# Moving the first chunk's quantisation into the scan's tail, a rounding step in PSUM, and attention's head before a stage boundary

## The chip, the cores and the metric

The kernel runs on one core of one Trainium2 chip. The metric is the device time of one execution in microseconds; the time before is 1036.28 us, the median of three runs (1035.46 to 1037.93).

## The reference

The input x has 8 sequences of 256 tokens with 128 features. Four residual blocks follow one another, each on a layer-normalised input:

```python
x = x + mamba4(layernorm(x))     # 4 mamba layers: projection, causal conv of 4 taps, silu,
                                 # selective scan h = exp(d*A)*h + d*u*B ; y = sum(h*C) + u*D,
                                 # y * silu(z), projection; 256 channels x 16 states
x = x + ffn(layernorm(x))
x = x + attention(layernorm(x))  # 16 heads of 8, causal, position bias, softmax, projection
x = x + ffn(layernorm(x))        # the same weights
```

The feed-forward block quantises to FP4 in blocks of 16 along the last dimension, the input, the weights and the hidden values:

```python
scale = max(abs(block)) / 6      # then nearest of 0, .5, 1, 1.5, 2, 3, 4, 6 with sign, times scale
gate, y = fp4(x) @ fp4(w_gate).T, fp4(x) @ fp4(w_up).T       # 352 columns each
out = fp4(silu(gate) * y) @ fp4(w_down).T
```

## The kernel before

All of x stays in SBUF (`resid`, 16 tiles of 128 tokens by 128 features). A chunk is four tiles (512 columns), a feed-forward step (k = 0 to 7) is two tiles (704 hidden columns). The kernel writes each engine's queue by hand; every engine works through its queue in order and waits on semaphores. The four stages are separate blocks, and an engine starts the next block after a barrier.

**The scan (`mamba_stage`).** There are 16 pairs of sequences-by-layer (n), each with 16 sub-steps (k). In a sub-step TensorE (PE) injects inputs into PSUM, ScalarE (ACT) computes four decays three sub-steps ahead, VectorE (DVE) runs four scans (L902), GpSimd (POOL) multiplies by C (L1002), and PE sums the products over the states into PSUM (L567). Behind sub-step 4 of the next pair DVE gates the result (`gating`, L911); for the last layer `add_out` (L917) adds the output projection to `resid` behind sub-step 9. After the last sub-step of the last pair, DVE computes the moments (L1038, L1042) of chunks 0 to 2 for the norm of FFN1, their offsets (L1065), then gates and adds the last output. ACT computes the reciprocal deviation (`scalar_rstd`: Ln and Exp) and normalises three chunks (L1073).

**The rounding (`Rounder`).** For one chunk or step: DVE takes peak (L1104), scale (L1106), reciprocal (L1108), a factor just below one (L1110); POOL multiplies (`pool_normal`, L1116); DVE takes the exponent bits (L1124); ACT makes the rounding step of them (L1130); DVE adds and subtracts it (`vector_round`, L1137 and L1139); POOL multiplies by the scale (`pool_dequant`, L1144). Value and step are SBUF tiles.

**FFN1 and FFN2 (`ffn_stage`).** Four x chunks are quantised, transposed by PE into a PSUM bank (L1360) and copied by ACT (L1423). Each tile has a gate matmul (L1370) and an up matmul (L1372), two banks each; ACT applies silu (L1430), DVE multiplies (L1270, `hidden`), then h is rounded, transposed (L1380), copied (L1435, L1436), multiplied by the down weights (L1390, two banks in turn) and added to `resid` by DVE (`add`, L1278). DVE rounds step k-2 and adds step k-5 during step k. In FFN2 three chunks of x are already quantised during attention; in FFN1 none is.

**Attention's head.** At the end of FFN1 chunk 0 is normalised and transposed for attention, and two of four groups of strips (`tensor_strips` L1617, `vector_strips` L1628) are computed. The other two groups and the values of chunk 0 (`project_v` L1707, `values` L1836), and POOL's constants (L1923 to L1927), stand at the head of the attention block, before the first scores (L1714, L1723).

Of the kernel before, what the change touches and what calls it, by code (L numbers as in the profile page):

```python
# [13 lines left out]
P = 128  # L14
F32 = mybir.dt.float32
BF16 = mybir.dt.bfloat16
# [203 lines left out]
def mamba_stage(core, x, w_xi, w_z, w_xp, w_dt, w_out, chan, ident_in, c_rows, diag_rows, w_ffn, norm):  # L220
# [3 lines left out]
    core.minus_step = core.sb("minus_step", [P, 1])  # L224
    with ExitStack() as stage:
# [87 lines left out]
        with nc.Block(no_gpsimd_drain=True) as block:  # L313
# [335 lines left out]
            def _(a):  # L649
# [142 lines left out]
                for n in range(NPAIR):  # L792
                    more = n + 1 < NPAIR
                    for k in range(SUBS):
# [10 lines left out]
                        if k == 13 and more:  # L805
                            read_dut(n + 1, 0)
                            read_dut(n + 1, 1)
                        decays(n * SUBS + k + 3)
# [21 lines left out]
                for c in range(PAIRS - 1):  # L830
                    norm.scalar_rstd(a, c)
                for c in range(PAIRS - 1):
                    norm.scalar_normalise(a, c)

            @block.vector
            def _(v):
# [81 lines left out]

                first_stats(0)
# [32 lines left out]
                for c in range(PAIRS - 1):  # L952
                    ring.wait_read(v, "out", NPAIR - PAIRS + c)
                    norm.vector_moments(v, c)
                for c in range(PAIRS - 1):
                    norm.vector_offset(v, c)
                gating(NPAIR - 1)
                add_out(NPAIR - 1)

            @block.gpsimd  # L960
            def _(p):
# [47 lines left out]
                for n in range(NPAIR):  # L1009
                    for k in range(SUBS):  # L1010
# [3 lines left out]
                        if k == 11 and n % PAIRS == 1 and lay(n) + 1 < DEPTH:  # L1014
                            layer_weights(lay(n) + 1)

# [61 lines left out]
class Rounder:  # L1078


    def __init__(self, core, sb, tag, blocks, depth=2):
        self.core, self.blocks, self.depth = core, blocks, depth
# [3 lines left out]
        self.value = sb(f"{tag}_value", [P, depth, blocks * BLK])  # L1086
# [6 lines left out]
        self.s_dequant = core.sem(f"{core.stage}_{tag}_dequantised")  # L1093

# [17 lines left out]
    def pool_normal(self, p, src, c):  # L1112
# [3 lines left out]
        self.core.nc.gpsimd.tensor_tensor(self.blocked(self.value[:, i, :]), src, self.spread(self.inv[:, i, :]),  # L1116
                                          ALU.mult).then_inc(self.s_normal, 1)

    def vector_exponent(self, v, c):
        i = c % self.depth  # L1120
        v.wait_ge(self.s_normal, c + 1)
        if c >= self.depth:
            self.s_round.wait(v, "rounded", c - self.depth)
        self.core.nc.vector.tensor_scalar(self.step[:, i, :].bitcast(U32), self.value[:, i, :].bitcast(U32), EXP_BITS, None,  # L1124
                                          ALU.bitwise_and).then_inc(self.s_exponent, 1)

    def scalar_step(self, a, c):
        i = c % self.depth
        a.wait_ge(self.s_exponent, c + 1)
        self.core.nc.scalar.activation(self.step[:, i, :], self.step[:, i, :], ACT.Relu, bias=self.core.minus_step[:, :],  # L1130
                                       scale=HALF_STEP).then_inc(self.s_step, 1)

    def vector_round(self, v, c):
        nc, i = self.core.nc, c % self.depth
        value, step = self.value[:, i, :], self.step[:, i, :]
# [972 lines left out]
```

## Time and profile before

| what | value |
|---|---|
| runs | 1035.46, 1036.28, 1037.93 us |
| the profiled execution | 1035.28 us |
| its span | 1033.6 us |
| busy: PE, DVE, ACT, POOL | 949.8, 902.6, 761.5, 760.9 us |
| scan, to the last add_out | up to 727.7 us |
| FFN1, to the last add | 728.1 to 802.4 us |
| attention | about 807 to 967 us |
| FFN2, to the last add | 967.6 to 1031.2 us |

The time of the execution holds the span and what lies around it. The stages' limits are read off the timeline at the lines named above. Busy shares are averages over stages with different limits, so each place that the change touches has to be read by itself.

### The profile page before, as it was taken

What the parts mean: (1) busy time and instruction counts of PE and PEld (TensorE: products, weight loads), DVE (VectorE), ACT (ScalarE), POOL (GpSimd) and SP (SyncE); (2) the same over time, 40 slices, a digit from 0 to 9 for tenths busy, and PEclk for the clock granted to TensorE, in tenths of its full rate; (3) what the DMA queues carried; (4) which work ended last, traced back from release to release, by engine and by line L of the source; (5) the groups of instructions that cost most, each with busy time, mean ns of one, the idle gap of its engine ahead of it and who ended that gap; (6) DMA issues with size and microseconds to landing.
All of it is one profiled execution on the core that took longest, in us unless ns stands there. A gap on an engine that the chain in (4) does not pass through costs nothing. (4 is left out here: it accounts for less than half of the span.)

```text
span 1033.6 us, 29750 instructions
## 1 busy us (share of the span) xinstructions
PE 949.8 (92%) x11909; PEld 580.2 (56%) x11909; DVE 902.6 (87%) x1724; ACT 761.5 (74%) x1683; POOL 760.9 (74%) x426
## 2 busy tenths in 40 slices
PE   5799999999999999999999999988477999999786
PEld 2455555565555555555555555655346566666456
DVE  6879998999989999899998999999699767787597
ACT  5888898988989889899898897984434255555442
POOL 1688999989999899999999989998254223333243
PEclk9799999999999999999999999999888999999888
DMA  6745453544535444454444544440571010000001
GB/s 187 254 160 166 137 173 125 166 147 162 167 128 164 147 165 146 145 167 146 165 146 138 158 147 159 147 132 14 128 155 21 21 23 17 7 2 2 1 0 41
DMA packets 69272, 120.88 MB, mean 117 GB/s; under 512 B 40072, under 2 KB 51152, under 8 KB 60112
## 3 DMA queue, kind: packets, MB, share of 16 engines
q1 hardware_dynamic: 69136, 118.98, 37.3%
q8 instruction: 95, 1.56, 0.6%
q14 instruction: 41, 0.34, 0.1%
HBM read 111.10 MB, written 6.29 MB: 114 GB/s over the span
## 5 line engine op out<-in xcount | busy, mean ns | idle before, releaser
L902 DVE TENSOR_TENSOR_SCAN hid<-decay,acc 128x256 f32<-128x256 f32 x1024 | 604.6, 664 | 40.9 <-PE acc L539 40.4
L1002 POOL TENSOR_TENSOR prod<-hid,c_rep 128x1024 f32<-128x1024 f32 x256 | 600.7, 2380 | 43.8 <-DVE hid L902 32.9
L765 ACT ACTIVATE decay<-delta,a_neg 128x255 f32<-128x255 f32 x1024 | 428.4, 502 | 47.6 <-DVE hid L902 47.4
L539 PE MATMUL acc<-b_diag,du_t 64*64 64x256 f32 x4096 | 273.1, 383 | 15.9 <-DVE hid L902 12.2
L567 PE MATMUL ring<-prod,ident 64*64 64x256 f32 x4096 | 255.5, 379 | 2.2 <-POOL prod L1002 2.2
L539 PEld LDWEIGHTS acc<-b_diag,du_t 64*64 64x64 f32 x4096 | 147.9, 134 | 124.8 <-DVE hid L902 55.3
L567 PEld LDWEIGHTS ring<-prod,ident 64*64 64x64 f32 x4096 | 152.0, 133 | 83.5 <-issue 22.7
L1916 POOL TENSOR_SCALAR_AFFINE_SELECT att_probs<-att_probs 128x512 f32<-128x512 f32 x64 | 41.1, 642 | 102.5 <-ACT att_probs L1959 100.1
L1959 ACT ACTIVATE att_probs<-acc 128x384 f32<-128x384 f32 x128 | 55.8, 488 | 52.5 <-PE acc L1733 52.5
L444 PE MATMUL ring<-xpad,diag_cw 64*64 64x512 f32 x512 | 60.5, 589 | 0.0
L1116 POOL TENSOR_TENSOR ffn_h_value<-ffn_h,ffn_h_inv 128x704 f32<-128x704 f32 x16 | 23.7, 1480 | 43.2 <-DVE ffn_h_value L1139 32.5
L1130 ACT ACTIVATE ffn_h_step<-ffn_h_step,minus_step 128x704 f32<-128x704 f32 x16 | 14.1, 883 | 54.7 <-DVE ffn_h_step L1124 54.7
L1731 PE MATMUL acc<-att_qk 17*128 17x256 f32 x256 | 53.2, 426 | 0.5 <-ACT att_probs L1959 0.4
L1723 PE MATMUL ring<-att_qk 17*128 17x256 f32 x256 | 47.3, 426 | 0.0
L1845 DVE TENSOR_REDUCE att_npk<-ring 128x2 f32<-128x512 f32 x64 | 43.7, 683 | 0.0
L1370 PE MATMUL ring<-wgT,ffn_xqT 128*128 128x352 f32 x64 | 30.0, 556 | 14.8 <-ACT ffn_silu L1430 9.2
L1844 DVE TENSOR_REDUCE att_npk<-ring 128x2 f32<-128x256 f32 x64 | 27.1, 423 | 16.6 <-PE ring L1722 16.3
L989 POOL TENSOR_TENSOR du<-delta,u 128x512 f32<-128x512 f32 x30 | 37.7, 1285 | 0.0
L1733 PE MATMUL acc<-att_qk 17*128 17x128 f32 x256 | 33.1, 269 | 0.0
L444 PEld LDWEIGHTS ring<-xpad,diag_cw 64*64 64x64 f32 x512 | 19.8, 133 | 22.6 <-issue 19.1
L427 PE MATMUL ring<-cur,wxi 128*128 128x512 f32 x60 | 31.5, 650 | 0.8 <-ACT cur L659 0.8
L1733 PEld LDWEIGHTS acc<-att_qk 17*128 17x128 f32 x256 | 31.7, 185 | 0.8
(180 smaller groups left out, 1263.7 us busy)
## 6 DMA issues: line engine op xcount, KB each, us to landing
c_rep<-c_rows SPq DMA_DIRECT2D x64, 1024.0 KB, 4.7
b_diag<-diag_rows SPq DMA_DIRECT2D x62, 512.0 KB, 3.9
diag_rows<-zeros SPq DMA_DIRECT2D x2, 2048.0 KB, 12.4
att_qk<-in_pos_q SPq DMA_DIRECT2D x4, 768.0 KB
att_qk<-in_pos_k SPq DMA_DIRECT2D x4, 768.0 KB
att_qk<-att_dense SPq DMA_DIRECT2D x24, 64.0 KB
resid<-in_x SPq DMA_DIRECT2D x4, 256.0 KB, 3.9
c_rows<-bc SPq DMA_DIRECT2D x64, 8.0 KB, 1.5
```

The costliest lines, as they stand in the source:

```text
L444: last = nc.tensor.matmul(out[h * HALF:(h + 1) * HALF, :], diag_cw[rows, lay(n) % 2, h, k, :], xpad[rows, h, :, k:k + SEQ], start=(k == 0) ...
L539: last = nc.tensor.matmul(inj[m * HALF:(m + 1) * HALF, K % 2, at:at + HALF * SG], du_t[rows, n % 2, e, chans:chans + HALF], b_diag[rows, K ...
L567: last = nc.tensor.matmul(y[h * HALF:(h + 1) * HALF, at], ident[rows, rows], prod[rows, H % PRODS, h, s, :], start=False, stop=(H % HSUMS ...
L765: last = nc.scalar.activation(decay[:, K % DECAYS, s, 1:], delta[:, n % 2, h, e * SEQ + 1:(e + 1) * SEQ], ACT.Exp, scale=a_neg[:, lay(n) % ...
L902: last = nc.vector.tensor_tensor_scan(hid[:, K % HIDS, s, :], decay[:, K % DECAYS, s, :], rows[:, s, :], 0.0, ALU.mult, ALU.add)
L1002: nc.gpsimd.tensor_tensor(prod[:, K // 2 % PRODS, h], hid[:, K % HIDS, :, :], c_rep[:, g, :, at], ALU.mult).then_inc(s_prod, 1)
L1723: return nc.tensor.matmul(out[:, P:SPAN], q[:, P:], k, start=False, stop=True, skip_group_check=True)
L1731: nc.tensor.matmul(out[:, 0:SEQ], k[:, 0:P], q, start=True, stop=True)
L1733: banks.fill(nc.tensor.matmul(out[:, SEQ:SPAN], k[:, P:], q[:, P:], start=True, stop=True), f"t{i}", u)
L1845: last = nc.vector.tensor_reduce(npk[:, g % 2, 1, at], score_bank(u)[:, :, P:SPAN], AX, ALU.max, negate=True)
L1916: nc.gpsimd.affine_select(at, at, [[0, 4], [1, P]], ALU.is_ge, zero, base=0, channel_multiplier=-1).then_inc(s_causal, 1)
L1959: banks.read(nc.scalar.activation(probs[:, g % 3, js[i], 0:SPAN], banks.bank(f"t{i}", u)[:, 0:SPAN], ACT.Exp, scale=SCALE), f"t{i}", u)
```

## The change

Nothing of what is computed changes. What moves is:

- **Scan's tail.** In the last pair DVE computes the moments of chunk 0 behind sub-step 6, the offset of chunk 0 behind 9, the moments of chunk 1 behind 12. Behind the last scan it quantises chunk 0 (its multiply on DVE, by a new `vector_normal`), with offset 1, the moments of chunk 2 and the rounding before the last gating. POOL dequantises chunk 0 at its queue's end.
- **Rounder.** The x chunks are rounded in place in `normed`. For h, ACT writes its step to PSUM (704 columns, one buffer), and so DVE's two rounding instructions read one operand from there.
- **FFN.** One gate bank rather than two; one down bank rather than two; the transposes of x and of h share a bank. DVE rounds step k-1 during step k, adds step k-4 between the maxima and the rounding, and takes the exponent of the step before ahead of the products. POOL's dequantisation waits for that exponent. In both stages ACT loads silu's table before it copies chunk 0.
- **Attention's head.** All four strip groups, the values of chunk 0 and POOL's constants stand at FFN1's end.

```diff
+                        if n == NPAIR - 1:
+                            if k in (6, 12):
+                                chunk_moments(k // 6 - 1)
+                            if k == 9:
+                                norm.vector_offset(v, 0)
+                first.vector_scales(v, 0)
+                first.vector_normal(v, 0)
+                first.q.vector_exponent(v, 0)
+                norm.vector_offset(v, 1)
+                chunk_moments(2)
+                first.q.vector_round(v, 0)
                 gating(NPAIR - 1)
+                norm.vector_offset(v, 2)
                 add_out(NPAIR - 1)
...
+    def vector_normal(self, v, src, c):
+        i = c % self.depth
+        self.s_scales.wait(v, "below", c)
+        need(v, self.s_dequant, c - self.depth + 1)
+        self.core.nc.vector.tensor_tensor(self.blocked(self.value(c)), src, self.spread(self.inv[:, i, :]),
                                           ALU.mult).then_inc(self.s_normal, 1)
...
     def scalar_step(self, a, c):
         i = c % self.depth
         a.wait_ge(self.s_exponent, c + 1)
-        self.core.nc.scalar.activation(self.step[:, i, :], self.step[:, i, :], ACT.Relu, bias=self.core.minus_step[:, :],
+        if self.held is not None and c:
+            self.s_round.wait(a, "rounded", c - 1)
+        self.core.nc.scalar.activation(self.steps(i), self.step[:, i, :], ACT.Relu, bias=self.core.minus_step[:, :],
...
-        gate_bank = [bank(ring, 1), bank(ring, 2)]
-        up_bank = [bank(ring, 3), bank(acc, 0)]
-        hT_bank = [bank(acc, 1)[:, 0:2 * P], bank(acc, 1)[:, 2 * P:4 * P], bank(acc, 2)[:, 0:2 * P]]
-        down_bank = [bank(acc, 3)[:, 0:2 * P], bank(ring, 0)[:, 0:2 * P]]
+        qh = Rounder(core, sb, "h", HCOLS // BLK, 4, acc[:, 2 * BANK:2 * BANK + HCOLS])
+        x_bank, gate_bank, up_bank = bank(ring, 0), bank(ring, 1), [bank(ring, 2), bank(acc, 0)]
+        hT_bank = [bank(ring, 0)[:, 0:2 * P], bank(ring, 0)[:, 2 * P:4 * P], bank(acc, 1)[:, 0:2 * P]]
+        down_bank = bank(ring, 3)[:, 0:2 * P]
...
+                norm.vector_moments(v, 3)
+                if early == 1:
                     x.vector_scales(v, 1)
+                    x.q.vector_exponent(v, 1)
                     x.vector_scales(v, 2)
+                norm.vector_offset(v, 3)
+                for k in range(HSTEPS + 1):
+                    if k >= 2:
+                        qh.vector_exponent(v, k - 1)
+                    if k == 2:
+                        x.q.vector_exponent(v, 3)
+                    if attention and k == HSTEPS - 1:
+                        v.wait_ge(s_add, 2)
+                        attention.norm.vector_moments(v, 0)
                     if k < HSTEPS:
                         hidden(k)
+                    if k >= 4:
+                        add(k - 4)
+                    if k == 0 and early == 1:
+                        x.q.vector_round(v, 1)
+                        x.q.vector_exponent(v, 2)
+                    if k == 1:
+                        qh.vector_exponent(v, 0)
                         x.vector_scales(v, 3)
+                    if attention and k == HSTEPS:
                         attention.norm.vector_normalise(v, 0)
+                    if k >= 1:
+                        qh.vector_round(v, k - 1)
+                    if k == 1 and early == 1:
+                        x.q.vector_round(v, 2)
+                    if k == 2:
+                        x.q.vector_round(v, 3)
...
+                for k in range(HSTEPS + 2):
+                    if k >= 2:
+                        p.wait_ge(qh.s_exponent, min(k, HSTEPS))
+                        h_dequant(k - 2)
+                    if k < HSTEPS:
+                        h_normal(k)
...
-                        need(t, s_silu, n - 1)
+                        need(t, s_silu, n)
...
-                    need(t, s_add, k - 1)
+                    need(t, s_add, k)
...
+                norm.scalar_rstd(a, 3)
+                nc.scalar.preload_act_table_set(SILU)
+                copy_x(0)
+                if early == 1:
                     x.q.scalar_step(a, 1)
                 gate(0)
+                norm.scalar_normalise(a, 3)
+                for k in range(HSTEPS + 2):
                     if 1 <= k <= HSTEPS:
                         qh.scalar_step(a, k - 1)
+                    if k == 0 and early == 1:
+                        x.q.scalar_step(a, 2)
...
-                for g in range(2, HGROUPS):
-                    tiles.tensor_strips(t, g)
-                project_v(0)
                 t.wait_ge(s_maskb, 2)
```

## Rows read from the trace of the kernel before

**Rows 1.** The page, part 1: busy us, share and instructions of each engine.
```profile
PE 949.8 (92%) x11909; PEld 580.2 (56%) x11909; DVE 902.6 (87%) x1724; ACT 761.5 (74%) x1683; POOL 760.9 (74%) x426
```

**Rows 2.** Timeline, scan's end: start us, us, engine, line, operation, out<-in, count, [idle before].
```profile
704.47 0.69 DVE L917 TENSOR_TENSOR resid<-resid,ring 128x512 f32<-128x512 f32 x1 [0.86 <-PE ring L514]
705.08 13.97 DVE L902 TENSOR_TENSOR_SCAN hid<-decay,acc 128x256 f32<-128x256 f32 x24
707.57 13.97 POOL L1002 TENSOR_TENSOR prod<-hid,c_rep 128x1024 f32<-128x1024 f32 x6 [1.45 <-DVE hid L902]
718.96 0.84 DVE L1038 BATCH_NORM_STATS2 stats<-resid 128x6 f32<-128x128 f32 x4
...
720.14 0.84 DVE L1038 BATCH_NORM_STATS2 stats<-resid 128x6 f32<-128x128 f32 x4
...
723.62 1.23 DVE L911 TENSOR_TENSOR yg<-ring,gate 128x1024 f32<-128x1024 f32 x1 [0.21 <-PE ring L567]
```

**Rows 3.** Timeline, one middle step of FFN2.
```profile
1006.82 1.39 POOL L1144 TENSOR_TENSOR ffn_hq<-ffn_h_value,ffn_h_scale 128x704 f32<-128x704 f32 x1
...
1007.55 0.70 DVE L1106 TENSOR_SCALAR ffn_h_scale<-ffn_h_peak 128x44 f32<-128x44 f32 x1
...
1008.84 0.52 DVE L1124 TENSOR_SCALAR ffn_h_step<-ffn_h_value 128x704 uint32<-128x704 uint32 x1
...
1009.28 0.88 DVE L1137 SCALAR_TENSOR_TENSOR ffn_h_value<-ffn_h_step,ffn_h_value 128x704 f32<-128x704 f32 x1
...
1011.17 1.39 POOL L1116 TENSOR_TENSOR ffn_h_value<-ffn_h,ffn_h_inv 128x704 f32<-128x704 f32 x1 [2.96 <-DVE ffn_h_value L1139]
1011.34 0.51 DVE L1270 TENSOR_TENSOR ffn_h<-ffn_silu,ring 128x352 f32<-128x352 f32 x1
...
1012.32 0.89 DVE L1104 TENSOR_REDUCE ffn_h_peak<-ffn_h 128x44 f32<-128x704 f32 x1
...
1013.24 0.70 DVE L1106 TENSOR_SCALAR ffn_h_scale<-ffn_h_peak 128x44 f32<-128x44 f32 x1
```

**Rows 4.** Timeline, attention: the offset beside POOL.
```profile
911.40 0.64 POOL L1916 TENSOR_SCALAR_AFFINE_SELECT att_probs<-att_probs 128x512 f32<-128x512 f32 x1 [1.87 <-ACT att_probs L1959]
...
911.70 0.36 DVE L1065 SCALAR_TENSOR_TENSOR ffn_offset<-meanvar,rstd 128x4 f32<-128x4 f32 x1
```

**Rows 5.** Timeline, the front of FFN1.
```profile
728.14 0.69 DVE L1104 TENSOR_REDUCE ffn_x_peak<-normed 128x32 f32<-128x512 f32 x1 [0.40 <-PEq L313]
...
729.56 0.86 DVE L1038 BATCH_NORM_STATS2 stats<-resid 128x6 f32<-128x128 f32 x4
...
731.20 0.20 ACT L1050 ACTIVATE rstd<-lnvar 128x4 f32<-128x4 f32 x1
...
733.63 1.28 ACT L1447 ACT_TABLE_LOAD   x1
...
736.76 0.60 ACT L1423 ACTIVATE ffn_xqT<-ring 128x512 f32<-128x512 f32 x1 [1.85 <-PE ring L1360]
...
740.16 0.46 ACT L1430 ACTIVATE ffn_silu<-ring 128x352 f32<-128x352 f32 x1 [2.19 <-PE ring L1372]
```

**Rows 6.** Timeline: FFN1's last add, FFN2's first DVE instruction and last add.
```profile
802.01 0.42 DVE L1278 TENSOR_TENSOR resid<-resid,ring 128x256 f32<-128x256 f32 x1 [0.46 <-PE ring L1390]
...
967.58 0.87 DVE L1038 BATCH_NORM_STATS2 stats<-resid 128x6 f32<-128x128 f32 x4 [0.39 <-PEq L1678]
...
1030.82 0.42 DVE L1278 TENSOR_TENSOR resid<-resid,ring 128x256 f32<-128x256 f32 x1 [0.92 <-PE ring L1390]
```

**Rows 7.** Timeline, FFN2's tail: down products on PE.
```profile
1024.52 2.77 PE L1390 MATMUL ring<-wdT,ffn_hqT 128*128 128x128 f32 x12
...
1029.28 1.50 PE L1390 MATMUL ring<-wdT,ffn_hqT 128*128 128x128 f32 x12
```

**Rows 8.** Windows: length, busy us (count) by engine, granted clock, DMA share, GB/s.
```profile
1000.00:1004.00 4.00, 3.86 (x21) 2.87 (x22) 3.86 (x8) 1.13 (x4) 2.52 (x2) 1.00 0.01 2
...
1024.00:1026.00 2.00, 2.00 (x11) 1.99 (x10) 1.14 (x2) 0.86 (x2) 1.05 (x1) 0.50 0.04 8
```

More of the change, by code:

```diff
@@ L807, in _ @@
                             read_dut(n + 1, 1)
+                        if k == 8 and not more:
+                            norm.scalar_rstd(a, 0)
                         decays(n * SUBS + k + 3)
@@ L829, in _ @@
                             a_rates(lay(n) + 1)
[L830 to L833, printed above, removed]
+                norm.scalar_normalise(a, 0)
+                norm.scalar_rstd(a, 1)
+                first.q.scalar_step(a, 0)
+                norm.scalar_normalise(a, 1)
+                norm.scalar_rstd(a, 2)
+                norm.scalar_normalise(a, 2)
             @block.vector
@@ L1085, in __init__ @@
         self.inv = sb(f"{tag}_inv", [P, depth, blocks])
-        self.value = sb(f"{tag}_value", [P, depth, blocks * BLK])
+        self.values = values or [self.value_tile(sb, tag, n) for n in range(depth)]
         self.step = sb(f"{tag}_step", [P, depth, blocks * BLK])
@@ L1152, in __init__ @@
         self.core, self.norm = core, norm
-        self.q = Rounder(core, sb, "x", CH // BLK)
-        self.xq = sb("xq", [P, CHUNKS, CH])
         self.normed = core.normed[:, :, :].rearrange("p t (b k) -> p (t b) k", k=BLK)
+        rows = core.normed[:, :, :].rearrange("p t d -> p (t d)")
+        self.q = Rounder(core, sb, "x", CH // BLK, values=[rows[:, c * CH:(c + 1) * CH] for c in range(CHUNKS)])
     def blocks(self, c):
@@ L1213, in scalar, with ffn_stage @@
         return last
-def ffn_stage(core, tag, norm, inputs=None, attention=None, out=None):
+def ffn_stage(core, tag, x, early, attention=None, out=None):
     nc, ring, acc, ident = core.nc, core.ring, core.acc, core.ident
@@ L1628, in vector_strips, with tensor_values, vector_values, pool_set @@
             banks.read(nc.vector.tensor_tensor(at, at, src, ALU.add), kind, 0)
+    def tensor_values(self, t, c):
+        nc, banks = self.core.nc, self.banks
+        banks.wait_free(t, "v", c)
+        banks.wait_read(t, "x", c)
+        for i in range(CH_TILES):
+            last = nc.tensor.matmul(banks.bank("v", c)[:, i * P:(i + 1) * P], self.xT[:, i * P:(i + 1) * P], self.wqkv[:, 2, :],
+                                    start=True, stop=True)
+        banks.fill(last, "v", c)
+    def vector_values(self, v, c):
+        nc, banks = self.core.nc, self.banks
+        banks.wait_filled(v, "v", c)
+        dst = self.vals[:, c * CH_TILES:(c + 1) * CH_TILES, :, 0:HD]
+        src = banks.bank("v", c).rearrange("p (t h d) -> p t h d", t=CH_TILES, d=HD)
+        bias = self.bv[:, :].rearrange("p (h d) -> p h d", d=HD).unsqueeze(1).broadcast_to([P, CH_TILES, HEADS, HD])
+        banks.read(nc.vector.tensor_tensor(dst, src, bias, ALU.add), "v", c)
+    def pool_set(self, p):
+        nc = self.core.nc
+        self.wait(p)
+        nc.gpsimd.tensor_copy(self.ident_b[:, :], self.core.ident[:, :]).then_inc(self.s_maskb, 1)
+        nc.gpsimd.tensor_copy(self.mask_b[:, :, :], self.mask[:, :].unsqueeze(1).broadcast_to([P, 2, P])).then_inc(self.s_maskb, 1)
+        nc.gpsimd.memset(self.npk[:, :, :, :], 0.0).then_inc(self.s_npk, 1)
+        nc.gpsimd.memset(self.vals[:, :, :, HD:HD + 1], 1.0).then_inc(self.s_ones, 1)
 def attention_stage(core, tiles, x):
```

228 lines of the change are left out of this document (86 added, 142 removed).

## The prediction

> **What bounds the kernel now.** I read the page's busy shares first: no engine fills the span, VectorE (DVE) has 902.6 us of 1033.6 [rows 1], so the answer lies in the stages. The edits touch three places: the last pass of the scan, the first feed-forward stage (FFN1) with its hand-over to attention, and the last one (FFN2). I then read the timeline of each.
>
> In the scan's end DVE and POOL run in lockstep. The last six sub-steps are 24 scans in 13.97 us, 2.33 us each, with no gap; POOL's six products take 13.97 us too, and start only after a scan [rows 2]. POOL's first product here starts 2.49 us after DVE's first scan, and its last ends at 721.54, 2.49 us after DVE's last scan at 719.05. So whatever is put between scans moves the end of the scan by its full length. Behind the scans, DVE computes the moments of chunks 0 to 2 while POOL's last product and TensorE's (PE's) last sums run; gating starts at 723.62, that is 4.57 us after the last scan, and it alone sets the end. Those moments are free today.
>
> In both FFN stages DVE is the bound of a middle step: from one scale instruction to the next is 5.69 us, with DVE never idle [rows 3]. In it lies a stall: the scale (128x44) takes 0.70 us where the exponent, sixteen times its size, takes 0.52. It ends at 1008.25, when POOL's dequantisation (1006.82 + 1.39 = 1008.21) has just ended. The same is seen on a four-element instruction in attention: it begins at 911.70 beside a POOL instruction and ends at 912.06, when POOL has just ended at 912.04 [rows 4]. The tensor_reduce, and the product with an operand in PSUM, keep their 0.89 and 0.51 us beside POOL [rows 3].
>
> **Part 1: chunk 0 quantised in the scan's tail.**
> Added between scans: moments(0) behind sub-step 6, offset(0) behind 9, moments(1) behind 12. One moments group is 1.18 us (718.96 to 720.14) [rows 2]; two are 2.4. The offset is a four-element instruction with both inputs in SBUF. POOL's product 9 starts when product 8 ends, about 0.15 us behind scan 9, and runs 2.33 us; after add_out (0.86 us of waiting, then about 0.6) the offset can start some 1.5 us behind scan 9 and by the attention rows waits for the product's end: about 1.0 us. If it didn't wait it would cost 0.15. I take 1.0, since the nearest row is the same instruction. Sum: the last scan ends 3.4 us later (bounds 2.5 and 3.6). ScalarE (ACT) gets a log and an exp of 0.5 us together in front of a decay; it is busy 74% of the span [rows 1], and I take nothing.
>
> Added between the last scan and gating: peak, scale, reciprocal, product, exponent, offset(1), moments(2), two roundings. The peak takes 0.7 us; the scale is then held until POOL's product ends, 2.49 us behind the scan. From there: scale, reciprocal and last factor about 0.65, the product of 512 columns 0.75 (the multiply of 704 columns that has two SBUF inputs takes 0.88 [rows 3]), exponent 0.5, offset 0.2, moments 1.2, roundings 1.5. That makes 7.1 us. Gating could have started at 4.57, so it is 2.5 us late. If nothing were held: 5.5 us, 0.9 late; were the roundings held by ACT's step too: 3.5 late. I take 2.5. Offset(2) goes behind gating, where DVE waits for PE.
> So FFN1 starts 3.4 + 2.5 = 5.9 us late (bounds 3.4 and 7.1).
>
> The Trainium skill's "SBUF — State Buffer", section "Who interferes with whom", says that VectorE and GpSimd share one port pair under an exclusive lock, which a VectorE instruction needs if it has two SBUF inputs or runs in a two-port mode; the loser waits for the whole instruction. By that rule offset(0) and the first scale wait as above; if the short rows were chance, the sum would be 3.4 instead of 5.9. The trace agrees with the rule in the rows named, and it is what speaks against this edit.
>
> **Part 2: FFN1's front.** Today from the stage's first DVE instruction (728.14) to the first silu (740.16) are 12.02 us, since chunk 0 is quantised there [rows 5]. After: moments(3), log and exp (729.56 to 731.40, 1.84 us), the table load (1.28), then copy of x to silu (736.76 to 740.16, 3.40): 6.5 us. Of the 5.9 lost, 5.5 come back here at first. But one gate bank means that the second tile's gate matmul waits for the first silu: 0.5 us of silu, then one tile on PE. At half clock such a tile is most of the 3.40 us from copy to silu, some 2.4; at full clock I take half of it, 1.2. The second silu comes some 2.5 to 3 us behind the first. It delays DVE by about 2.1 us at the first step and 1.5 at the second. And the order of queues holds more: ACT's step of chunk 2 stands before the gates of step 1, and waits for an exponent which stands behind the first step and the rounding of chunk 1.
>
> **Part 3: the middle steps.** With the step in PSUM both roundings have one SBUF input and run beside POOL. POOL's dequantisation is let go by the exponent, runs 1.39 us under two products and the peak (1.9 us of DVE), and its next multiply under add and roundings; so the scale no longer stalls: 5.69 - 0.51 = 5.18 us a step. PSUM operands cost nothing extra in the rows that exist (352 columns 0.51, 704 in SBUF 0.88); ACT's write of 704 columns to PSUM isn't shown. Its nearest rows are SBUF writes of 0.88, and it has over 1 us of slack either way, so I take no cost. PE is the narrow place: in the middle of FFN2 it is listed busy 3.86 of 4.00 us at full clock [rows 8], with ends that are modelled. By count a step is four tile products of 0.6 us, six transposes and twelve down instructions (1.50 [rows 7]), about 4.7 us, and the wait for silu adds 0.6. I take it that this fits beside 5.18; if it doesn't, steps stay at today's 5.7 and both stages lose 2 us each of what follows.
> FFN1 by sum: a chunk of x costs DVE 1.42 for its scales (728.14 to 729.56) [rows 5], and by columns about 0.4 for the exponent and 1.5 for the roundings, 3.3. DVE work: 8 x 5.18 + 3 chunks at 3.3 + 3 moments at 1.25 + one normalise about 1.1 = 56.1. Waits: POOL's multiply of chunk 1 1.25; silus 3.0 in step 0 and 2.8 in step 1; DVE held by POOL 1.0, 0.65, 0.8, 0.25 (chunk 1's rounding, chunk 3's scale and exponent, the scale of step 3) and 1.2 (attention's normalise beside the dequantisation of step 6); the end behind the last rounding 3.6 beyond its adds; 0.9 small change. Together 15.5, and 0.7 for half-clock matmuls in the tail: 72.3 us. Today 728.14 to 802.43 are 74.3 [rows 5, 6]. Gain 2.0.
>
> **Part 4: the end of FFN1 and attention's head.** One bank for the down product puts add(6) between down(6) and down(7), about 0.5 us, counted above. The four strip groups and the values move before the stage boundary; PE runs them without today's gap, but the boundary then waits for DVE's values. PE's matmuls are the same; I take -0.2 (bounds -1.5, if the gap is saved whole, and 0.5). POOL's memsets and casts were not awaited.
>
> **Part 5: FFN2.** The work is 8 x 5.18 + moments 1.3 + one chunk 3.3 = 46.0. Copy of x now stands behind the table load, so the first silu is at 6.5 us from 967.58: waits 5.8, then 2.5 and 1.15 for the second silus; stalls 0.9; ACT's last step 0.6; the end (dequantisation 1.4, transposes 0.9, down 1.4, add, down 1.4) 4.9 beyond adds; 0.6 small change. That is 62.4. In the tail PE is mostly idle, and there the granted clock is already 0.50 today (1.2 GHz), 1.00 (2.4 GHz) in the middle [rows 8]; a down product takes 2.77 at the one level, 1.50 at the other [rows 7]. I add 1.4 for part of that: 63.8, against 63.66 today [rows 6]. No gain: fewer stalls pay for the serial down bank, later silus and a tail in sequence.
>
> **Sum:** 5.9 - 2.0 - 0.2 + 0.1 = +3.8 us. The profiled execution took 1035.28 us for its span of 1033.6; after: 1039.1. The median of the three is 1.0 above that execution, so the forecast is 1040.
>
> **Rivals.**
> A. VectorE isn't held by POOL's products in the scan's tail (3.4 us lost rather than 5.9), the fronts' second silus come at full clock (-1 each), the tail isn't slow (-1.4), and the early steps, which are longer than 5.69 today, gain another 2. 3.8 - 2.5 - 2 - 1.4 - 2 = -4: 1032. For it: there is more than one stall to lose in the steps with a chunk of x; against it: both held rows [rows 3, 4], and the lockstep, in which nothing added to DVE is covered. Decides: whether DVE's small SBUF instructions wait for POOL's products.
> B. PE is thinned. The single gate bank spreads the matmuls until the clock is granted at 1.2 GHz in middle steps as well. A step's PE work at that level is 4.7 x 2.77 / 1.50 = 8.7 us against DVE's 5.18, 3.5 more; three such steps in the two stages, partly covered, add 5 beyond the forecast: 1045. For it: clock 0.50 in the tail with similar gaps [rows 8]; against it: PE is busy over nine tenths of a middle step. The Trainium skill, "TensorE: Matmul & The Clock Gate", Part 1, has the clock fall when PE has been idle and return only after sustained work; it is by this rule that B could happen, and the rows show both levels.
> C. Everything cancels: scan +5, FFN stages -5: 1036. For it: FFN1's front gives back 5.5 of the 5.9 at once, and only silus and queue order take it away.
>
> **How the numbers follow.** Forecast with its own range 1038.4 to 1043: 0.45; A (faster) 0.22; C 0.20; B 0.13. A measurement tells from no change what is over 0.2%, about 2 us. Faster 0.22 is A; same 0.20 is C; slower 0.58 is forecast and B. The range 1034 to 1043.5 leaves out the far part of A and B.
>
> **What would show it.** Right: last scan at about 722.5, a gap of 7 us to gating, DVE's offset(0) some 1 us long in that pass; FFN1's first DVE instruction near 734; first silu 6.5 us behind it; middle steps of 5.2 us; first scores 3 to 4 us later than today; FFN2 of 63 to 65 us. Wrong: gating within 5 us of the last scan, or FFN stages under 70 and 61 us.

## Result, and the profile after

The changed kernel takes 1055.93 us (median of 4 runs, 1055.38 to 1056.52), the kernel before beside it 1035.87 (4 runs): a ratio of 1.0196, 95% interval 1.018 to 1.0212. That is 20 us slower. The direction of the forecast (1040) holds, its size does not, and the time lies 12 us above the upper end of its range. The profiled span is 1054.3 us, 20.7 above that of before.

Part 1 of the page, which answers to [rows 1]: DVE has 8 us less than before, ACT 1.7 more, POOL 1.6 less; only PE stands out, with 21 us more for the same 11909 instructions. The line under it is PE's granted clock in 40 slices of the span, in tenths.

```profile
PE 970.8 (92%) x11909; PEld 583.7 (55%) x11909; DVE 894.4 (85%) x1725; ACT 763.2 (72%) x1683; POOL 759.3 (72%) x425
...
PEclk9799999999999999999999999998588899999569
```

The same line of the kernel before; its two weak places, the FFN stages, are now deeper:

```profile
PEclk9799999999999999999999999999888999999888
```

The scan's end in the timeline of the kernel after, against [rows 2]:

```profile
706.28 1.03 DVE L1082 SCALAR_TENSOR_TENSOR ffn_offset<-meanvar,rstd 128x4 f32<-128x4 f32 x1
...
722.67 0.66 DVE L1127 TENSOR_REDUCE ffn_x_peak<-normed 128x32 f32<-128x512 f32 x1
723.37 1.85 DVE L1129 TENSOR_SCALAR ffn_x_scale<-ffn_x_peak 128x32 f32<-128x32 f32 x1
...
729.50 1.22 DVE L915 TENSOR_TENSOR yg<-ring,gate 128x1024 f32<-128x1024 f32 x1
```

Up to gating the forecast came true: the scans end at 722.7 rather than 719.05, the small offset takes 1.03 us, the scale waits for POOL's product (1.85), and gating is 6.8 us behind the scans. Gating starts 5.9 us later than before, as predicted. FFN1's first DVE instruction is 7.4 us late (735.60 against 728.14): the out product behind gating takes 3.62 us at the lower clock, before it took 2.02.

The front of FFN2, PE, ACT and DVE in one order (the front of FFN1 looks the same), with the clock of two stretches:

```profile
985.35 1.54 PE L1406 MATMUL ring<-wgT,ffn_xqT 128*128 128x352 f32 x2 [2.73 <-ACT ffn_xqT L1459]
986.69 1.38 PE L1408 MATMUL ring<-wuT,ffn_xqT 128*128 128x352 f32 x2
988.11 0.46 ACT L1466 ACTIVATE ffn_silu<-ring 128x352 f32<-128x352 f32 x1 [2.81 <-PE ring L1408]
988.60 0.52 DVE L1307 TENSOR_TENSOR ffn_h<-ffn_silu,ring 128x352 f32<-128x352 f32 x1 [4.94 <-ACT ffn_silu L1466]
988.62 1.54 PE L1406 MATMUL ring<-wgT,ffn_xqT 128*128 128x352 f32 x2 [0.55 <-ACT ffn_silu L1466]
989.96 1.38 PE L1408 MATMUL acc<-wuT,ffn_xqT 128*128 128x352 f32 x2
991.37 0.46 ACT L1466 ACTIVATE ffn_silu<-ring 128x352 f32<-128x352 f32 x1 [2.81 <-PE acc L1408]
```

```profile
986.00:990.00 4.00, 3.45 (x7) 1.56 (x6) 0.52 (x1) 0.46 (x1) 0.00 (x0) 0.50 0.00 0
...
1006.00:1010.00 4.00, 3.35 (x5) 1.68 (x6) 3.83 (x9) 1.80 (x3) 2.25 (x2) 0.50 0.00 0
```

Read the chain: gate matmul 1.54, up matmul 1.38, silu 0.46, and only then the next tile's gate matmul. A tile takes 3.26 us, a step of two tiles over 6.5, more than DVE's work of 5.18. PE is busy 3.4 of 4 us and yet at the lower of its two levels (0.50, 1.2 GHz) from about 973 to 1017.5; it stops for 0.55 us or more at every tile. In the kernel before the second tile needs no silu, and there PE runs through; the clock rises inside this stretch, and the second up matmul already takes 0.76:

```profile
969.35 1.54 PE L1370 MATMUL ring<-wgT,ffn_xqT 128*128 128x352 f32 x2 [0.69 <-ACT ffn_xqT L1423]
970.68 1.38 PE L1372 MATMUL ring<-wuT,ffn_xqT 128*128 128x352 f32 x2
971.86 1.26 PE L1370 MATMUL ring<-wgT,ffn_xqT 128*128 128x352 f32 x2
972.96 0.76 PE L1372 MATMUL acc<-wuT,ffn_xqT 128*128 128x352 f32 x2
```

The last additions, against [rows 6]:

```profile
981.53 0.87 DVE L1055 BATCH_NORM_STATS2 stats<-resid 128x6 f32<-128x128 f32 x4 [0.39 <-PEq L1737]
...
1051.60 0.42 DVE L1315 TENSOR_TENSOR resid<-resid,ring 128x256 f32<-128x256 f32 x1 [1.76 <-PE ring L1425]
```

All profiled executions, cut at the same marks, in us. "Entry" runs from the gating of the pass before the last (690.85 before) to FFN1's first DVE instruction; "units" from attention's first peak to its last but one; "exit" from there to FFN2's first DVE instruction; FFN1 and FFN2 to the start of their last addition. In e6, e9, e12 and e13 the rounding of chunk 0 stands before FFN1's first DVE instruction, and so in the entry. Between FFN1 and units lie 11.0 us in every kernel.

| kernel | entry | FFN1 | units | exit | FFN2 |
|---|---|---|---|---|---|
| before | 37.3 | 73.9 | 141.2 | 13.4 | 63.2 |
| after | 44.7 | 75.4 | 144.3 | 15.2 | 70.1 |
| e1 | 44.6 | 77.7 | 141.2 | 15.1 | 68.1 |
| e2 | 44.5 | 81.5 | 148.6 | 14.5 | 74.1 |
| e3 | 39.8 | 82.9 | 141.2 | 13.1 | 74.5 |
| e4 | 42.7 | 74.0 | 141.2 | 15.0 | 59.7 |
| e5 | 43.6 | 71.8 | 141.2 | 15.0 | 60.7 |
| e6 | 39.6 | 72.5 | 141.2 | 15.0 | 59.7 |
| e7 | 38.5 | 74.9 | 141.2 | 14.8 | 62.7 |
| e8 | 44.7 | 78.8 | - | 13.2 | 68.0 |
| e9 | 41.2 | 67.2 | 144.3 | 15.3 | 61.7 |
| e10 | 44.5 | 76.5 | 141.3 | 15.0 | 71.8 |
| e11 | 44.5 | 73.0 | 141.2 | 15.0 | 62.1 |
| e12 | 40.9 | 73.8 | 144.3 | 15.4 | 69.8 |
| e13 | 39.6 | 67.4 | 141.2 | 13.5 | 59.7 |
| e14 | 37.3 | 75.5 | 141.2 | 14.7 | 62.0 |

Of the 20.7 us, 7.4 are lost at the entry, 1.5 in FFN1, 3.1 and 1.8 at attention's edges, and 6.9 in FFN2. (The profiled execution of e8 is the slow one of its four, with a lower clock in the first part of attention, so its units are left out and its ratio is that of the other three.)

### The profile page after: what moved, and what is told of

Read it like the earlier page. It is cut to its first block and busy times, and to the rows that moved or that the text cites. A ratio compares the mean times of both kernels' runs of the same rounds, so it can differ in the third digit from the quotient of the medians.

```text
span 1054.3 us, 29765 instructions
## 1 busy us (share of the span) xinstructions
PE 970.8 (92%) x11909; PEld 583.7 (55%) x11909; DVE 894.4 (85%) x1725; ACT 763.2 (72%) x1683; POOL 759.3 (72%) x425
## 5 line engine op out<-in xcount | busy, mean ns | idle before, releaser
L906 DVE TENSOR_TENSOR_SCAN hid<-decay,acc 128x256 f32<-128x256 f32 x1024 | 604.9, 663 | 41.2 <-PE acc L539 40.7
L539 PE MATMUL acc<-b_diag,du_t 64*64 64x256 f32 x4096 | 273.6, 383 | 17.6 <-DVE hid L906 13.9
L1954 POOL TENSOR_SCALAR_AFFINE_SELECT att_probs<-att_probs 128x512 f32<-128x512 f32 x64 | 40.9, 639 | 102.8 <-ACT att_probs L1992 100.4
L444 PE MATMUL ring<-xpad,diag_cw 64*64 64x512 f32 x512 | 60.7, 590 | 0.0
L1406 PE MATMUL ring<-wgT,ffn_xqT 128*128 128x352 f32 x64 | 38.1, 688 | 22.1 <-ACT ffn_silu L1466 14.7
L1466 ACT ACTIVATE ffn_silu<-ring 128x352 f32<-128x352 f32 x32 | 14.8, 462 | 49.7 <-PE acc L1408 34.8
L1180 POOL TENSOR_TENSOR ffn_hq<-ffn_h_value,ffn_h_scale 128x704 f32<-128x704 f32 x16 | 22.4, 1403 | 19.1 <-DVE ffn_h_step L1154 14.9
L1406 PEld LDWEIGHTS ring<-wgT,ffn_xqT 128*128 128x128 f32 x64 | 13.0, 254 | 40.9 <-ACT ffn_silu L1466 25.4
L1784 PE MATMUL acc<-att_qk 17*128 17x128 f32 x256 | 33.1, 269 | 0.0
```

The lines of the kernel that those rows point to most:

```text
L444: last = nc.tensor.matmul(out[h * HALF:(h + 1) * HALF, :], diag_cw[rows, lay(n) % 2, h, k, :], xpad[rows, h, :, k:k + SEQ], start=(k == 0) ...
L539: last = nc.tensor.matmul(inj[m * HALF:(m + 1) * HALF, K % 2, at:at + HALF * SG], du_t[rows, n % 2, e, chans:chans + HALF], b_diag[rows, K ...
L906: last = nc.vector.tensor_tensor_scan(hid[:, K % HIDS, s, :], decay[:, K % DECAYS, s, :], rows[:, s, :], 0.0, ALU.mult, ALU.add)
L1406: nc.tensor.matmul(gate_bank[:, 0:FFN], at, core.wgT[:, 0:FFN], start=True, stop=True)
L1954: nc.gpsimd.affine_select(at, at, [[0, 4], [1, P]], ALU.is_ge, zero, base=0, channel_multiplier=-1).then_inc(s_causal, 1)
```

## The experiments

**e1, e2: the gate bank and the step, each undone in the kernel after.** e2 puts the step back into SBUF; e1 does so and gives the gates two banks.

```
- qh = Rounder(core, sb, "h", HCOLS // BLK, 4, acc[:, 2 * BANK:2 * BANK + HCOLS])
+ qh = Rounder(core, sb, "h", HCOLS // BLK, 4)
  (e1 also)
- need(t, s_silu, n)
+ need(t, s_silu, n - 1)
- nc.tensor.matmul(gate_bank[:, 0:FFN], ...)
+ nc.tensor.matmul(gate_bank[i][:, 0:FFN], ...)
```

> The changed kernel with two gate banks again; to make room, the rounding step of h goes back to SBUF. Theory (the single gate bank makes the gate, up, silu chain serial, PE idles in every tile, the clock is granted at 1.2 GHz for over 30 us in each feed-forward front, and that is most of the loss): the clock rises within 6 us of each front, FFN2 takes 62 to 66 us instead of 70.5, FFN1 68 to 72 instead of 75.8, total 1040 to 1045. Rival (the loss comes from the new order of the queues and the moved work, not from the bank): total stays within 3 us of 1056.

> The changed kernel with the rounding step of h in SBUF, one gate bank kept; it differs from the run with two gate banks in the gate bank alone. Theory (the bank decides): 1056 or up to 6 us slower, because both roundings have two SBUF inputs and meet POOL's multiply; the clock stays at 0.50 in both fronts. Rival (the step in PSUM is itself harmful): clearly faster than 1056, toward 1045.

Measured: e1 1053.33 us (1.0171 [1.0156, 1.0187]), e2 1066.9 (1.0312 [1.0271, 1.0353]). Both miss what was expected, and e1 lies where its rival had it: two gate banks alone don't win back the 20 us. Its clock rises in FFN2 and falls again (0.99 from 990 to 1000 us, 0.52 from 1000 to 1010), and its later steps take 6.26 us from one first product to the next. e2 against e1 is 13.6 us by the medians; the table has 3.8 of it in FFN1 and 6.0 in FFN2, where the gate bank acts, and 7.4 in attention, where e2's clock was down (0.84 from 810 to 835, 0.78 from 835 to 860) and e1's was not. Taking the step out of PSUM costs some 11 us (e2 against the kernel after), with the same reserve. So this pair doesn't settle the cause, and two gate banks with the step in PSUM were not tried; e3 and e4 do more, and e8 tells what e1's step in SBUF costs.

**e3: the single gate bank alone, in the kernel before.**

```
- gate_bank = [bank(ring, 1), bank(ring, 2)]
+ gate_bank = [bank(ring, 1), bank(ring, 1)]
- need(t, s_silu, n - 1)
+ need(t, s_silu, n)
```

> The kernel before with nothing changed but one gate bank instead of two. Theory: the fronts run at 1.2 GHz for many us longer and the kernel loses 8 to 16 us (1044 to 1052). Rival (the serial wait alone costs, the clock does not follow): 1 to 4 us lost, clock as in the kernel before.

Measured: 1056.51 us (1.0204 [1.0179, 1.0228]), 21.6 above the kernel before beside it (1034.95), more than the 8 to 16 expected. One bank name loses as much as the whole change: FFN1 +9.0, FFN2 +11.3. (The entry's +2.5 lies in code that e3 doesn't touch.) No filler was tried on this kernel, so what the clock and what the serial chain cost here isn't shown apart. The clock of its FFN2 front, which swings:

```profile
977.70:987.70 10.00, 7.81 (x18) 4.46 (x19) 4.07 (x16) 5.25 (x11) 1.06 (x1) 0.51 0.00 1
987.70:997.70 10.00, 6.24 (x16) 2.87 (x14) 5.11 (x12) 2.34 (x5) 2.98 (x2) 0.83 0.01 2
997.70:1007.70 10.00, 6.76 (x14) 3.40 (x13) 6.23 (x12) 3.37 (x6) 2.73 (x2) 0.50 0.00 0
```

**e4: the clock held up, all else as in the kernel after.** Transposes of the identity into the down bank, which is free until the first down product: ten behind the first chunk's transposes, two in front of each wait for a silu in steps 0 to 3. They change no dependence; they only give PE something to do where it waits.

```
+ def warm(count):
+     for _ in range(count):
+         nc.tensor.transpose(bank(ring, 3)[:, 0:P], ident[:, :], ident[:, :])
  turn_x(0)
+ warm(10)
  gate_up(0)
  ...
+ if 0 < n and k < 4:
+     warm(2)
  need(t, s_silu, n)
```

> The changed kernel plus idle-time work for PE: ten transposes of the identity behind the first transposes of x, and two in front of each wait for silu in steps 0 to 3, into a PSUM bank that nothing reads then. Theory (clock): the granted clock is 1.00 from about 5 us into each front, the second silu follows the first by 1.9 instead of 3.3 us, FFN2 takes 63 to 66 us, total 1042 to 1047. Rival (the serial chain costs the same at either clock, or PE work is the bound): no gain or slower than 1056, since PE has more to do.

Measured: 1036.92 us (1.0026 [1.001, 1.0042]): from a ratio of 1.0196 to 1.0026, which is 17.6 us, better than expected. Not all of it can be the filler's. From the gating of the pass before the last to the end of the span, where the start of an execution plays no part, e4 is 17.0 us shorter than the kernel after. Of these, 2.0 lie at the entry, before any filler has run: the same out product took 2.02 us in e4 and 3.62 in the kernel after.

```profile
727.36 2.02 PE L514 MATMUL ring<-wo,yg 128*128 128x128 f32 x16 [2.27 <-DVE yg L915]
```

Another 3.1 lie in attention's first units; they take 144.3 us also in e9, which has the filler, and 141.3 in e10, which has not. What stands where the filler acts is 10.4 us in FFN2 and 1.4 in FFN1. The rows of FFN2's front show the same chain as in the kernel after, now with a tile every 2.00 us:

```profile
972.62 2.29 PE L1401 MATMUL ring<-ident 128*128 128x128 f32 x10
975.56 0.86 PE L1412 MATMUL ring<-wgT,ffn_xqT 128*128 128x352 f32 x2 [0.64 <-ACT ffn_xqT L1466]
976.25 0.76 PE L1414 MATMUL ring<-wuT,ffn_xqT 128*128 128x352 f32 x2
976.85 0.38 PE L1401 MATMUL ring<-ident 128*128 128x128 f32 x2
977.56 0.86 PE L1412 MATMUL ring<-wgT,ffn_xqT 128*128 128x352 f32 x2 [0.33 <-ACT ffn_silu L1473]
```

```profile
972.00:974.00 2.00, 2.00 (x11) 2.00 (x11) 1.16 (x9) 0.89 (x3) 0.00 (x0) 0.50 0.04 8
974.00:976.00 2.00, 1.36 (x7) 0.90 (x6) 0.00 (x0) 1.49 (x2) 0.00 (x0) 0.82 0.00 0
976.00:986.00 10.00, 8.29 (x34) 4.85 (x32) 5.46 (x13) 3.96 (x9) 1.41 (x2) 1.00 0.00 0
```

FFN2 takes 59.7 us, 3.5 less than before; its middle steps go by 5.17 us (from one first product to the next, 1001.93 to 1007.10), where the forecast had 5.18. In these middle steps the single bank costs nothing once the clock is up: DVE's own work fills them. The first step takes 4.01 us from one scale to the next, against 2.80 in the kernel before.

**e5, e6: the scan's tail on top of e4.** e5 puts all of the added work behind the last scan and in front of gating; e6 leaves only moments and two offsets in front of gating.

```
  (e6; both: nothing between the scans)
+ chunk_moments(0); chunk_moments(1)
+ norm.vector_offset(v, 0); chunk_moments(2); norm.vector_offset(v, 1)
  gating(NPAIR - 1)
+ first.vector_scales(v, 0); first.vector_normal(v, 0)
+ first.q.vector_exponent(v, 0); norm.vector_offset(v, 2)
  add_out(NPAIR - 1)
+ first.q.vector_round(v, 0)
```

> The kernel after with the filler of the earlier run (transposes of the identity into a free bank, which kept PE's clock at 1.00 in the fronts), and nothing between the last scans: the moments of chunks 0 and 1 and offset(0) stand behind the last scan, the quantisation of chunk 0 still before gating. It tells the lockstep from the quantisation. Time is counted from gating of the pass before (690.85 before, 690.88 after, 687.78 with the filler), since whole executions differ by some 4 us near their start. With the filler the last scan ended 31.5 behind it (28.2 before), gating stood at 38.2 (32.8 before). My theory (whatever stands between scans moves the scan by its length, and what stands behind them costs what it takes beyond the free 4.57 us): scan's end at 28.2 again, gating at 36.6, the time 1.6 us below the filler alone (1036.92), so about 1035.3. Rival (ACT's queue or POOL's products set the scan's end, not DVE's instructions): scan's end stays near 31.5 and the time is that of the filler plus 3.

> As the run before, but gating stands directly behind the moments, and chunk 0 is quantised behind gating, where DVE waits for PE's out product; its rounding stands behind the last addition. My theory: gating at 32.8 behind the gating of the pass before, as in the kernel before; FFN1's first DVE instruction at about 39 rather than 42.7, and the first silu about 4 us earlier than with the filler alone; time 1033 to 1034, below both kernels. Rival (PE, which now idles from its last sums until out, drops to the lower clock and pays it back, or the rounding behind the addition makes the first silu late): no more than 1 us below the run before.

Measured: e5 1037.9 us (1.0029 [1.0014, 1.0045]), e6 1034.89 (1.0002 [0.998, 1.0023]). In e5 the scans end 28.2 us behind the gating of the pass before, as in the kernel before, and gating stands at 37.3 (expected 36.6): the lockstep is confirmed. But the time did not fall as expected (1035.3), and one row says where it went:

```profile
727.43 1.22 DVE L914 TENSOR_TENSOR yg<-ring,gate 128x1024 f32<-128x1024 f32 x1
...
728.79 3.75 PE L514 MATMUL ring<-wo,yg 128*128 128x128 f32 x16 [5.96 <-DVE yg L914]
```

PE had been idle for 5.96 us, and its out product took 3.75 us instead of the 2.02 that it takes at the upper clock; the kernel after has the same (3.62). A long stop alone doesn't decide it in each execution. Of the eight that quantise chunk 0 before gating, seven have the product at 3.4 to 3.8 us and one (e4) at 2.02; of the four with e6's order none is slow; of the four with the scan of the kernel before one is (e3, 3.65). e6 gates nearly as early as the kernel before (33.1 us behind the gating before it, 32.8 there), PE keeps its clock, and the entry is 39.6: 3.1 us won on e4. Its time is 0.9 above the expected range.

**e7: the filler in the kernel before.** The same transposes, into the bank of its first down product.

> The kernel before with the same filler and nothing else of the change (transposes of the identity into a bank that is free until the first down product: ten behind the first chunk's transposes, two in front of each wait for a silu in steps 0 to 3). It asks how much of what the filler gained is owed to the single gate bank. Theory: the kernel before already reaches the upper clock at once in both fronts (740.8 and 972.9), so the filler can gain at most the 3 us or so that the matmuls of the first step take longer: 1033 to 1035.5, and the 19 us that the filler gained on the kernel after were the change's own loss. Rival: the fronts of the kernel before are slowed by the clock as well, and the filler gains 5 us or more, 1030 or less.

Measured: 1037.01 us (1.0015 [1.0004, 1.0027]): it gains nothing and may lose a little, though its mean clock is 0.82 in FFN1 and 0.86 in FFN2. What the filler gives back to the kernel after is the change's own loss.

**e8: e4 with the step of h in SBUF.** The first edit of e2.

> The kernel after with the filler, and the rounding step of h in SBUF again. It measures what the step in PSUM is worth where the clock is up, since in the run without filler that was mixed with the clock. Theory (POOL's multiply holds the roundings when both their operands are in SBUF): middle steps 6.2 us rather than 5.2, FFN1 about 81 rather than 74.0, FFN2 about 67.5 rather than 59.7, time about 1052. Rival (the 11 us seen without filler were mostly the clock): middle steps 5.5 or less and a time under 1042.

Measured: four times from 1054.22 to 1070.87 us, ratio 1.0214 [1.0183, 1.0244] against 1.0026 for e4, some 19 us. The table places 13.1 of them in the stages (FFN1 +4.8, FFN2 +8.3), where the step acts; the rest no trace places. FFN2 takes 68.0 us; a step 6.25, and the row to read is the first rounding, held until POOL's multiply is over:

```profile
1034.29 1.39 POOL L1139 TENSOR_TENSOR ffn_h_value<-ffn_h,ffn_h_inv 128x704 f32<-128x704 f32 x1 [1.30 <-DVE ffn_h_inv L1133]
1034.45 1.97 DVE L1173 SCALAR_TENSOR_TENSOR ffn_h_value<-ffn_h_step,ffn_h_value 128x704 f32<-128x704 f32 x1
1036.46 0.89 DVE L1175 SCALAR_TENSOR_TENSOR ffn_h_value<-ffn_h_value,ffn_h_step 128x704 f32<-128x704 f32 x1
```

**e9: ACT's order, on top of e6.** In e6 ACT waits for the exponent of chunk 2 with ready gates behind it:

```profile
743.76 0.72 ACT L1163 ACTIVATE ffn_x_step<-ffn_x_step,minus_step 128x512 f32<-128x512 f32 x1 [3.61 <-DVE ffn_x_step L1151]
744.39 0.44 ACT L1470 ACTIVATE ffn_silu<-ring 128x352 f32<-128x352 f32 x1
```

```
- if k == 0 and early == 1:
-     x.q.scalar_step(a, 2)
  if k + 1 < HSTEPS:
      gate(k + 1)
+ if k == 0 and early == 1:
+     x.q.scalar_step(a, 2)
```

> The run with filler and chunk 0 quantised behind gating (1034.89), and one more thing: on ACT the gates of step 1 stand in front of the step of chunk 2. There, without this, ACT idled 3.61 us and PE 4.54 us (740.35 to 744.89) for an exponent that DVE reaches only behind the first step and the rounding of chunk 1, and the second step's second product stood at 748.14. Theory (the order of ACT's queue costs FFN1 its idle time there): the product comes near 744.5, FFN1 is 3 to 4 us shorter (70 rather than 73.7), the time about 1031.5, below both kernels. Rival (DVE makes up for it later, since the step of chunk 2 comes later and with it chunks 2 and 3): FFN1 within 1 us of 73.7, time 1034 to 1035.

Measured: 1033.11 us (0.9987 [0.9973, 1.0001]), not the 1031.5 expected, and even with the kernel before. FFN1 falls from 72.5 to 67.2, more than expected, but in this execution attention's start ran at 0.50 (units 144.3), where that of e6 did not.

**e10: the same order alone in the kernel after. e11: only the filler at the waits. e12: e9 without filler.**

> The kernel after with that edit alone: no filler, chunk 0 where the change put it. It asks whether it is this gap of 4.5 us on PE, rather than the single gate bank, that keeps the clock at 0.50 in FFN1's front. Theory (the gate bank does: each tile's gate matmul waits for the silu of the tile before): the clock still rises near 770 and FFN1 gains only the order's 2 to 4 us; FFN2, where there is no such order, keeps its 70.1; time about 1052 to 1054. Rival (the gap does): the clock rises before 755, FFN1 shortens by 6 us or more and attention's first units by 3, time 1046 or less.

> The kernel after with the filler in front of the silu waits alone, without the ten transposes behind the first chunk's. It tells which part of the filler carries it: the start (PE idle 2.3 us for the copy of the first chunk) or the gaps between tiles that the single bank makes. Theory (the gaps): the clock rises within two steps of each front and the time is within 4 us of the 1036.92 of the full filler. Rival (a front that starts at 0.50 stays there as long as any gap is left): near 1050.

> All edits of the first run of this call but no filler at all: chunk 0 quantised behind gating, gates of step 1 first. What the filler is worth on the better order. Theory: the single gate bank still holds the clock down in FFN2's front (FFN2 near 70) and in part of FFN1's; time 1045 to 1051. Rival (the better order is enough): within 3 us of the run with filler.

Measured: e10 1052.08 (1.0167 [1.0146, 1.0188]); e11 1043.2 (1.0085 [1.0054, 1.0115]), two near 1040 and two at 1045.5; e12 1047.48 (1.0117 [1.01, 1.0135]). In e10 the clock stays at 0.50 over most of 738 to 776 without the gap: the gap is not what holds it down. In e11 it rises some 9 us into FFN2, and the time lies between the two theories, so both parts of the filler count. e12 against e9 is the cleanest measure of the filler, since attention took the same in both: 14.4 us, of which the table has 6.6 in FFN1 and 8.1 in FFN2. Twenty us of FFN2, from its tenth on, first in e12, then in e9:

```profile
983.00:1003.00 20.00, 16.58 (x28) 8.14 (x29) 15.33 (x31) 6.97 (x14) 7.01 (x6) 0.50 0.00 1
```

```profile
979.00:999.00 20.00, 13.98 (x55) 8.04 (x56) 18.00 (x37) 9.64 (x19) 9.54 (x7) 1.00 0.00 0
```

**e13, e14: the filler at all places, in the best version and in the kernel before.** Added to e9: eight transposes before attention's first turn, three before each turn of h in the tails, eight behind attention's first values, three before each late piece of attention.

```
  t.wait_ge(s_h, 2 * HSTEPS)
+ warm(8, gate_bank)
  attention.tensor_turn(t)
+ if k >= HSTEPS:
+     t.wait_ge(s_silu, 2 * HSTEPS)
+     warm(3, gate_bank)
  ...
  attention.tensor_values(t, 0)
+ attention.banks.wait_read(t, "q0", 0)
+ warm(8, bank(ring, 0))
  ...
+ if u >= UNITS:
+     for _ in range(3):
+         nc.tensor.transpose(core.ring[:, 0:P], ident[:, :], ident[:, :])
```

> The best version so far (1033.11) with the filler in the remaining places where the clock was seen at 0.50: eight transposes in front of attention's first turn and three in front of the turns of h in both tails (into the gate bank, free by then), eight behind attention's first values, and three in front of each late piece of attention's last iterations. Theory (the clock at attention's edges costs 3.1 us at its start and some 2 at its end, by chance in some executions): attention's units always take 141.2, its end 13.1 or less, FFN2 59.7; time 1028 to 1030. Rival (the filler stands in front of dependent work and costs what it gains, each transpose some 0.12 us): 1032 to 1034.

> The kernel before with the filler in the same places, apart from that behind attention's values. If the clock at the edges is chance that hits both kernels, it gains the same 2 to 3 us: 1032 to 1034, still above the run before. Rival (its fronts and tails have nothing to gain, as with the filler of its fronts alone): 1035 to 1037.

Measured: e13 1028.54 us (0.9926 [0.9898, 0.9953]), faster than both kernels; e14 1036.92 (1.0005 [0.9991, 1.0019]), as its rival had it: the kernel before gains nothing. In e13 the units take 141.2, the exit 13.5 (13.1 or less was expected) and FFN2 59.7. Its clock by slices, and a stretch of the exit and front that was at 0.50 in the kernel after:

```profile
PEclk9899999999999999999999999999988999999999
```

```profile
966.00:976.00 10.00, 6.90 (x28) 4.05 (x27) 3.39 (x10) 5.31 (x11) 0.99 (x1) 1.00 0.00 0
```

## Why the prediction was wrong, by its own steps

**Right.** Up to gating: the scan's end 3.7 us late (3.4 predicted), the offset 1.03 us, gating 6.8 behind the scans (7.1), 5.9 us late in all. (The terms given for the 7.1 add up to 7.3.) e5 confirms the lockstep by undoing it. But FFN1's first instruction is 7.4 us late, beyond the bound of 7.1, since no term allowed for the out product at the lower clock. The first silu stands 6.8 us behind FFN1's first DVE instruction (6.5). Middle steps of 5.18 us exist in the kernel after, one in FFN1 and two in FFN2, and e4 has them in both stages from its fourth step on, in FFN1 up to its last two. Attention's head moved nothing.

**Failed: the assumption of Part 3 that PE's 4.7 us and the silu waits "fit beside 5.18".** That count was made at the upper clock. It holds there: a tile takes 2.00 us in e4, two take 4.0. At the lower clock a tile takes 3.26, and the kernel stayed there for the first 36 us of FFN2 (981.5 to 1017.5): its first four steps take 6.6, 7.5, 6.6 and 8.9 us from one gate matmul to the next. FFN2, which was to be even (+0.1), lost 6.9. The stop of 0.55 us at each tile is what the single bank adds. The forecast's second silu "2.5 to 3 us behind the first" (3.26) used the lower clock, but only for the first step or two.

**Rival B named the mechanism and mis-sized it.** It was given three slow steps, 5 us and a chance of 0.13. With the filler 11.8 us come back in the two stages (after against e4: 10.4 in FFN2, 1.4 in FFN1), and 14.7 on the better order (e12 against e9). The price of a step was not too low (8.7 us of PE work, where 6.6 to 8.9 were measured); the slow steps were too few, and too much was taken as covered. Some 2 us at the entry and 3.1 in attention's first units went with a lower clock as well. But the out product is as slow in e3, whose scan is that of the kernel before, and fast in e4; the units take 144.3 with the filler in e9, and 141.3 without it in e10. Whether the change makes either likelier stays open. The argument against B, that PE is busy over nine tenths of a middle step, was the mistake: that was read from a stretch with two gate banks at the upper clock [rows 8]. In the kernel after PE is busy 86% of a stretch and the clock still doesn't rise. The Trainium skill, "TensorE: Matmul & The Clock Gate", section "A second HAM failure mode: psum-queue depth-cycling", describes short stops between groups of matmuls, owed to the use of PSUM banks, that make the clock swing; the rows here agree that such stops matter: the clock swings so in e3, and in the kernel after it doesn't swing but stays down.

**The small terms.** FFN1 was to gain 2.0; with the filler it gains nothing (74.0 in e4) until ACT's order is mended (72.5 in e6, 67.2 in e9), a queue order that the forecast named ("the order of queues holds more") and put at little. From one scale to the next its first two steps take 9.47 and 9.68 us in the kernel after and in e4 alike, so the clock doesn't set them; in e9 the first takes 5.41. FFN2 was to be even and is 3.5 us shorter with the filler. The forecast had 1.4 for a tail at the lower clock, and e4's tail has 1.00; the rest isn't placed. With the filler the change as a whole loses 0.26% (e4), within the forecast's own range by its ratio. Counted from the gating of the pass before the last it is +3.7 us, next to the forecast's +3.8, and that is luck: 5.4 at the entry, 0.1 in FFN1, 1.6 at the exit and -3.5 in FFN2, where the forecast had 5.9, -2.0, nothing and 0.1.

The exit's 15.0 against 13.4 us need not be the change's: the kernel before has 14.8 in e7, where only the filler is added, and 13.1 in e3. What decides at which moment the clock falls there stays open.

## What to carry to other kernels

Before a double-buffered PSUM bank is given up, follow the chain that it leaves (matmul, its reader, next matmul) at both clock levels; a count at the upper level alone hides a factor of nearly two. A few idle transposes where PE waits are a cheap test of whether the clock is the cause, and here also the cure: 14.4 us (e12 against e9). Where two engines run in lockstep, move work behind the event that both wait for, and behind the instruction that a third engine needs next.

## What the runs showed of the hardware that was not expected

PE busy for 3.45 of 4.00 us, with stops of 0.55 to 0.78 us, had the clock at 0.50 from 986 to 1017; in the kernel before it rose within a stretch that PE ran through (969.35 to 974), and in the kernel after, too, it rose at last in such a stretch (1013.69 to 1017.5). Not each such stretch raised it: PE ran from 995.22 to 998.79, too, and it stayed at 0.50. And it stayed up with more idle time than that: in e4 PE is busy 12.32 of the 18.00 us from 982 to 1000, and the clock is 1.00. Behind a stop of 5.96 us a product that takes 2.02 us elsewhere took 3.75.

The clock can rise on transposes alone: in e4 it rose between 974 and 976, when PE had run nothing but fourteen transposes since the stage began. The Trainium skill's "TensorE: Matmul & The Clock Gate", "Part 4: PE-mode transpose", says that the upper level doesn't engage for a matmul in transpose mode; these rows, in float32, speak against it, with one reserve: the profile lists these transposes as MATMUL and doesn't name the mode.

Executions of one kernel differ by 4 us near their start: the first gating starts at 89.3 to 89.8 us (e4, e7, e11, e12) or at 92.3 to 94.4 (all others). Between 50 and 60 us the granted clock is 1.00 in e4, and 0.77 in the kernel before, 0.75 in the kernel after, 0.89 in e3. The times of e4 fall in two groups, 1035.8 to 1037.2 and 1040.2 to 1040.8, which would fit it; only one of its executions was profiled.
